# Attention weights loaded during the experts, split ahead of h, and the class norm solved together with tiles 0 to 3

## The chip, the core and the metric

The kernel runs on one core of a Trainium2 chip. A core has five engines, each with its own queue of instructions: TensorE (PE in the rows; its weight loads are PEld), VectorE (DVE), ScalarE (ACT), GpSimd (POOL) and SyncE (SP). They meet only through semaphores. Sixteen DMA engines serve all queues. The metric is the device time of one execution in microseconds (us).

## The reference

The program is a small vision tower with two layers. It works on h, 16 sequences of 129 rows (one class row and 128 tokens) of 512 numbers in float32.

```python
h = tokens of a state-space kernel, with the class row in front
h = h + scan_attention(layernorm(h))          # layer 0
h = h + experts(layernorm(h), H=256)          # layer 0: 8 experts, top 2, one shared expert
h = h + gla(layernorm(h))                     # layer 1, this case
h = h + experts(layernorm(h), I=352)          # layer 1
```

The change lies where the first line of experts ends and the line of `gla` begins. Of the latter:

```python
q = silu(x @ Wq.T) * SCALE
k_sig = sigmoid(x @ Wk.T)
gf = log_sigmoid(-k_sig)
o = gla(q, k_sig, x, gf)                      # a gated linear recurrence over the row index
go = o @ Wog.T + x @ Wig.T
rms = o * rsqrt(mean(o * o) + EPS) * g_weight
out = rms * go * sigmoid(go)
```

Here x is the layernorm of h. Wog and Wig are 512 x 512.

## The kernel before

h lies in the chip's memory as 17 tiles: tile n (0 to 15) holds the 128 tokens of sequence n, one to a partition, and tile 16 (`NB`) holds the 16 class rows. Each stage is a function that returns one piece of program for each engine; `tower` strings these together, so each engine runs the stages in the order tokenizer, scan, first experts (`ffn_layer`, "ffn0"), gated linear attention (`gla_layer`), second experts. The order of the work is thus the order of the code on each engine, and no scheduler changes it.

**The end of the first experts.** Rows are sorted by expert into 40 tiles (`NTILE`) of 128 slots. For each slot tile GpSimd gathers the rows, TensorE makes the products, VectorE scales the result, and GpSimd adds it with an accumulating scatter (L1514) into h in DRAM (`h_rows`). The semaphore `ffn0_e_down` counts the slot tiles that TensorE has finished. Expert weights lie over the place of the old norm output and beyond; SyncE loads experts 2 to 7 one after another (L990, L992) and then, as each pair has landed, counts up a semaphore that releases it. `stored` (L1139 to L1144) makes SyncE wait until the last scatter has landed in DRAM.

**The start of the attention.** SyncE (`sync` of `gla_layer`) first waits for the last product of the experts, since the weights wqk, wog, wig and the mask lie over memory that the experts used, then issues five loads, then waits in `stored`, and then loads h back: class rows first (L1847), then four quarters of four tiles (L1849). VectorE clears its buffers, copies three small pieces (`own`, L1862), and takes the norm in the groups of L1831: class tile, tiles 0 to 3, 4 to 9, 10 to 15. For each group it takes statistics (L495), aggregates (L519), solves the inverse root in nine dependent steps on all columns of the group (`newton`, L529 to L539) and applies the result tile by tile (L544), which counts up `gla_xn_ready`. TensorE turns each tile (L555) in that order and projects (L2112) the class rows and the quarters to queries and keys; ScalarE evacuates the turned tiles (L2029) and makes the bands (L2035 to L2042).

**The split.** For near-float32 products wog and wig are split in two parts: a rounded one, made by ScalarE (`s.activation(to[:, 0], w, ACT.Copy)`, L2017), and the rest, made by VectorE (a subtraction, L1877). Before, ScalarE does this first of all in the stage, and VectorE after all four groups of the norm. The first user is TensorE's `xw_of(0)`, which waits for all four parts (`gla_weights_split` 4).

Memory: `gla_raw` holds the unsplit weights and the mask, `gla_rounded` the parts and what else is rounded. Both begin at `y_at` before, `gla_raw` first.

## Time and profile before

| | |
|---|---|
| time, median of 3 runs | 1547.92 us (1547.54 to 1548.44) |
| the profiled execution | 1549.41 us, of which span 1547.6 us |
| PE busy | 1385.4 us, 90% of the span |
| PEld busy | 1078.2 us, 70% |
| DVE busy | 832.9 us, 54% |
| POOL busy | 483.6 us, 31% |
| ACT busy | 378.7 us, 24% |
| chain that ended last | PE 80%, DVE 11%, issue 3%, DMA 2%, ACT 2% |
| mean granted TensorE clock | 0.973 |

The span is the time from the first to the last record of the profile; what the execution's time has more lies around it. The busy shares are averages over stages that differ much. The chain follows the last instruction back, at each step to what released it, so it tells at each moment which engine the end of the program depended on. TensorE holds the chain over most of the run, with gaps at the seams between stages. The seam of this case lies between 600 and 700 us of the span.

### The profile page before, as it was taken

To read this page: it belongs to the slowest core of one execution; us is meant where nothing else is said; L and a number is where in the kernel's file an instruction comes from. 1 tells how busy PE (TensorE), PEld (TensorE's weight loads), DVE (VectorE), ACT (ScalarE), POOL (GpSimd) and SP (SyncE) were. 2 spreads that over 40 slices of the span, in tenths; PEclk is the share of its full clock that TensorE was granted. 3 is DMA by queue.
4 is the path that set the end of the run, shared out by engine and by line. 5 is a ranking of instruction groups with operands and counts; after the bars stand their busy time and mean duration, and the time that the engine had idled before them with its cause. 6 is when DMAs were issued, how large, how long until landed. Compare 5 with 4: busy or idle time off the path is not lost.

```text
span 1547.6 us, 21953 instructions
## 1 busy us (share of the span) xinstructions
PE 1385.4 (90%) x6469; PEld 1078.2 (70%) x6470; DVE 832.9 (54%) x1692; ACT 378.7 (24%) x738; POOL 483.6 (31%) x350
## 2 busy tenths in 40 slices
PE   0586939999999999389998989999999989999997
PEld 0584427888444444147776778888888879999996
DVE  8985898555222222663657765555555543333332
ACT  3114133121111111242223312333332212222221
POOL 0651530450344443001111035533323213343332
PEclk9999969999999999699999999999999999999999
DMA  4592007103955554600000504666665679676443
GB/s 102 112 153 24 1 22 266 34 10 116 342 93 89 89 94 62 195 22 1 1 0 1 185 21 133 204 215 209 216 224 200 222 272 372 208 206 187 75 74 42
DMA packets 88403, 197.04 MB, mean 127 GB/s; under 512 B 28256, under 2 KB 32224, under 8 KB 84832
## 3 DMA queue, kind: packets, MB, share of 16 engines
q1 hardware_dynamic: 68240, 154.20, 30.8%
q0 software_dynamic: 20096, 42.02, 14.7%
q8 instruction: 33, 0.54, 0.1%
q14 instruction: 34, 0.28, 0.1%
HBM read 112.24 MB, written 81.02 MB: 125 GB/s over the span
## 4 chain that ended last, share of the span: by engine, by line
PE 80%; DVE 11%; issue 3%; DMA 2%; ACT 2%; POOLq 1%; POOL 0%; DVEq 0%; SPq 0%; ACTq 0%
PE ps L1616 25%; PE ps L1676 19%; PE ps L1738 9%; PE ps L2143 6%; PE ps L1764 4%; PE ps L442 4%; PE ps L1706 2%; PE ps L555 2%; DVE held L495 1%; PE ps L1752 1%; PE ps L2112 1%; PE ps L2168 1%; PE ps L861 1%; PE ps L862 1%; DVE held L1383 1%
## 5 line engine op out<-in xcount | busy, mean ns | idle before, releaser
L1676 PE MATMUL ps<-moe_rounded 128*128 128x384 f32 (+2 forms) x1800 | 375.3, 351 | 0.0
L1676 PEld LDWEIGHTS ps<-moe_rounded 128*128 128x128 f32 x1800 | 326.9, 188 | 33.4
L1383 DVE SCALAR_TENSOR_TENSOR held<-ps,moe_scratch,held 128x512 f32<-128x512 f32 (+1 forms) x255 | 187.4, 747 | 180.0 <-PE ps L1616 179.2
L1616 PE MATMUL ps<-moe_expert_parts,moe_rows_parts 128*128 (+1 forms) x1320 | 256.5, 347 | 3.1 <-DVE moe_rows_parts L1407 1.5
L1616 PE MATMUL ps<-moe_rounded 128*128 128x512 f32 (+3 forms) x885 | 241.8, 393 | 11.8 <-DVE moe_rounded L1365 9.7
L1616 PEld LDWEIGHTS ps<-moe_expert_parts,moe_rows_parts 128*128 128x128 f32 (+1 forms) x1320 | 217.5, 188 | 16.3 <-issue 4.1
L1616 PEld LDWEIGHTS ps<-moe_rounded 128*128 128x128 f32 (+2 forms) x885 | 146.5, 171 | 50.7 <-DVE moe_rounded L1365 12.0
L1393 DVE TENSOR_TENSOR moe_scratch<-moe_scratch,ps 128x256 f32<-128x256 f32 (+1 forms) x80 | 37.7, 471 | 237.4 <-ACT moe_scratch L1598 237.4
L1738 PE MATMUL ps<-moe_experts,moe_scratch 128*128 x320 | 144.2, 593 | 0.6 <-issue 0.6
L1487 POOL TENSOR_TENSOR moe_split_parts<-moe_scratch,moe_split_parts 128x704 fp32r<-128x704 f32 (+2 forms) x48 | 88.8, 1855 | 172.8 <-ACT moe_split_parts L1580 172.8
L1471 POOL DMA_INDIRECT slot_tokens<-moe_scratch x68 | 73.5, 1081 | 173.2 <-DVE held L1383 165.9
L1598 ACT ACTIVATE moe_scratch<-ps 128x256 f32<-128x256 f32 (+1 forms) x80 | 33.9, 424 | 331.3 <-PE ps L1738 193.0
L1567 ACT ACTIVATE moe_scratch<-ps 128x384 f32<-128x384 f32 (+2 forms) x75 | 38.7, 515 | 307.7 <-PE ps L1676 298.5
L442 PE MATMUL ps<-sb 128*128 128x64 f32 x256 | 56.5, 422 | 54.6 <-DVE sb L367 54.3
L2143 PE MATMUL ps<-gla_rounded 128*128 128x512 f32 (+1 forms) x408 | 101.5, 406 | 2.1 <-ACT gla_rounded L2066 2.1
L1738 PEld LDWEIGHTS ps<-moe_experts,moe_scratch 128*128 128x128 f32 x320 | 57.7, 190 | 58.8 <-issue 58.8
L442 PEld LDWEIGHTS ps<-sb 128*128 128x128 f32 x256 | 55.2, 332 | 55.4 <-POOL sb L392 54.0
L2143 PEld LDWEIGHTS ps<-gla_rounded 128*128 128x128 f32 (+1 forms) x408 | 75.2, 187 | 22.2 <-issue 2.6
L2012 POOL TENSOR_TENSOR moe_xn<-moe_scratch 128x512 f32<-128x512 f32 (+1 forms) x17 | 25.6, 1506 | 195.7 <-DVE moe_scratch L1946 195.7
L555 PE MATMUL ps<-held,moe_xn 128*128 128x128 f32 (+1 forms) x272 | 40.4, 293 | 51.3 <-DVE moe_xn L544 45.7
L555 PEld LDWEIGHTS ps<-held,moe_xn 128*128 128x128 f32 (+1 forms) x272 | 33.7, 153 | 65.5 <-issue 31.4
L1764 PE MATMUL ps<-moe_experts,moe_scratch 128*128 x160 | 75.4, 593 | 1.1 <-DVE moe_scratch L1415 1.1
(315 smaller groups left out, 1690.1 us busy)
## 6 DMA issues: line engine op xcount, KB each, us to landing
moe_expert_parts<-expert_parts SPq DMA_DIRECT2D x8, 3840.0 KB, 13.0
expert_parts<-moe_split_parts SPq DMA_DIRECT2D x32, 704.0 KB
moe_scratch<-in_ffn_gate_up SPq DMA_DIRECT2D x32, 352.0 KB, 4.3
xn_rows<-moe_xn SPq DMA_DIRECT2D x2, 4096.0 KB, 13.0
moe_experts<-in_ffn_gate_up SPq DMA_DIRECT2D x8, 1024.0 KB, 15.5
expert_parts<-moe_split_parts SPq DMA_DIRECT2D x8, 1024.0 KB
moe_scratch<-in_ffn_sh_gate_up SPq DMA_DIRECT2D x15, 512.0 KB, 3.5
tokens<-sb SPq DMA_DIRECT2D x16, 256.0 KB
```

The costliest lines, as they stand in the source:

```text
L442: mm = t.matmul(o, ub[:, u, hh, :], bb[:, u, hh, :], start=True, stop=True)
L555: ins = t_eng.transpose(ps_bank[:, k * r:(k + 1) * r], xn[0:r, t, k * P:(k + 1) * P], ident[0:r, 0:r])
L1383: v.scalar_tensor_tensor(out=hb[0:rows, t, :], in0=ps[0:rows, ADDED[t % 3], :], scalar=sg[0:rows, t:t + 1], in1=hb[0:rows, t, :], op0=ALU. ...
L1393: v.tensor_tensor(ehid[:, u], esil[:, u], e_up(u), ALU.mult).then_inc(ehr, 1)
L1471: p.indirect_dma_start(out=slots, out_offset=bass.IndirectOffsetOnAxis(ap=pos_u[0:r, j, t:t + 1], axis=0), in_=tab_u[0:r, t, j, :], in_off ...
L1487: p.tensor_tensor(part[0:rows, x, 1, 0:w], raw[0:rows, x, 0:w], part[0:rows, x, 0, 0:w], ALU.subtract).then_inc(plr, 1)
L1567: s.activation(unit_sil(u, m), unit_banks(u, m)[0], ACT.Silu).then_inc(silr, 1)
L1616: mm = t.matmul(out, lhs(k, x), rhs(k, y), start=(k == 0 and i == 0), stop=(k == ks - 1 and i == 2))
L1676: mm = t.matmul(unit_banks(u, m)[j], weights(k, x, j), xT[y][:, k, unit_cols(m)], start=(k == 0 and i == 0), stop=(k == KD - 1 and i == 2))
L1738: mm = t.matmul(ps[:, u, 0:2 * F], xgT[:, u, k], exg(e, k, 0, 2 * F), start=(k == 0), stop=(k == KD - 1))
L1764: mm = t.matmul(ps[:, 6 + u, :], ehT[0:FR[f], u, f, :], exd(e, f, FR[f]), start=(f == 0), stop=(f == NF - 1))
L2143: mm = t.matmul(out[0:r], xT[:, j % 2, x, k, 0:r], w[:, y, k, :], start=(k == 0 and i == 0), stop=(stop and k == KD - 1 and i == 2))
```

## The change

Five edits, all at this seam:

1. The loads of wqk, wog, wig and the mask become a function `weights`, which SyncE runs inside the first experts' stage, right behind the load of expert 7 (`beside(sp)`), and no longer after the last product. The load of `g_weight` stays in `sync` and goes behind the five loads of h.
2. For that, `gla_raw` moves to memory that no expert weight uses, just below the scratch area, and `gla_rounded` takes its place at `y_at`.
3. ScalarE waits for four loads in place of five, and for the last product of the experts, before it writes the rounded parts.
4. VectorE does the two subtractions ahead of the norm.
5. The norm's groups are class tile and tiles 0 to 3 together, 4 to 9, 10 to 15. The tiles of the first group are no contiguous range, so its nine steps run on all 17 columns.

```diff
--- before.py
+++ after.py
@@ -518,7 +518,7 @@
             r = tile_rows(t)
             c.put(v.bn_aggr(self.mv[0:r, t, :], self.stats[0:r, t, :]))
         c.wait()
-        cols = slice(tiles[0], tiles[-1] + 1)
+        cols = slice(tiles[0], tiles[-1] + 1) if tiles[-1] >= tiles[0] else slice(0, T)
         self.newton(v, c, self.mv[:, cols, 1], 1.0, eps, cols)
 
     NEWTON = 9
@@ -886,7 +886,7 @@
     return rows[0:NTOK, :].rearrange("(b s) d -> s b d", s=SEQ)
 
 
-def ffn_layer(nc, sem, sb, ps, d, dram, g, name, F, NSH, before, xr, made, split_w):
+def ffn_layer(nc, sem, sb, ps, d, dram, g, name, F, NSH, before, xr, made, split_w, beside=None):
 
 
 
@@ -1132,6 +1132,7 @@
         else:
             for e in range(2, NE):
                 load_expert(sp, e, e_in[e // 2])
+            beside(sp)
             for k in range(1, NE // 2):
                 sp.wait_ge(e_in[k], 2 * 16 * WD)
                 sp.sem_inc(rt, 1)
@@ -1788,7 +1789,7 @@
     return sync, vector, gpsimd, scalar, tensor, stored, ed
 
 
-def gla_layer(nc, sem, sb, ps, d, hd, h_in, h_got, g, before, stored, xr_next, rest):
+def gla_layer(nc, sem, sb, ps, d, hd, h_in, h_got, g, before, experts_done, stored, xr_next, rest):
 
 
 
@@ -1799,10 +1800,10 @@
     KH, BL, NBL, NG = 32, 32, 4, 4
     ROWS3 = 2 * KH + NB
     xn = Arena(g.low).take(T, D)
-    raw = Arena(g.gla_raw, g.y_at, g.y_at)
+    raw = Arena(g.gla_raw, g.gla_raw_at, g.gla_raw_at)
     wqk, wog, wig = raw.take(KD, 2 * KH), raw.take(KD, D), raw.take(KD, D)
     mask = raw.take(P)
-    f = Arena(g.gla_rounded, raw.at, raw.at)
+    f = Arena(g.gla_rounded, g.y_at, g.y_at)
     wo, wi = f.take(2, KD, D), f.take(2, KD, D)
     xT = f.take(2, 2, KD, P)
     atcF, xc3, xwc3, accF = f.take(NB, P), f.take(D), f.take(D), f.take(NG * P)
@@ -1810,7 +1811,7 @@
     kb = a.take(NBL, NG, SEQ)
     qr, sq, kk, av, bv, pv = (a.take(NG, SEQ) for _ in range(6))
     kcz, own, ss, xg16 = a.take(NBL, ROWS3), a.take(NB), a.take(T), a.take(KD, NB)
-    assert a.at <= g.high_at
+    assert a.at <= g.gla_raw_at
     a = Arena(g.high, g.high_at, g.high_at)
     xg = a.take(2, KD, QC)
     sg, pb, xw, ats, junk, gw = a.take(2, D), a.take(2, D), a.take(2, D), a.take(2, P), a.take(D), a.take(D)
@@ -1828,25 +1829,28 @@
     hr = sem("gla_h_ready")
 
     ORDER = [NB] + list(range(NB))
-    GROUPS = ([NB], range(0, 4), range(4, 10), range(10, NB))
+    GROUPS = (ORDER[0:5], ORDER[5:11], ORDER[11:T])
     TB1, CLS_BANK, QK_BANKS = (0, 1, 2), 3, (4, 5, 6, 7)
     TB2, XW_BANK, AT_BANK, ACC_BANK, O_BANKS, G_BANKS = (0, 1), 2, 3, 5, (4, 5), (6, 7)
     C3_ALL = 8
     bands = [slice(KH * q, KH * q + KH) for q in range(NG)]
     rows_of = (lambda n: NB if n == NB else P)
 
-    def sync(sp):
-        before(sp)
+    def weights(sp):
         sp.dma_start(wqk, d["Wqk"]).then_inc(w_in, 16)
         sp.dma_start(wog, d["Wog"].rearrange("(k p) n -> p k n", p=P)).then_inc(w_in, 16)
         sp.dma_start(wig, d["Wig"].rearrange("(k p) n -> p k n", p=P)).then_inc(w_in, 16)
-        sp.dma_start(gw, d["g_weight"].partition_broadcast(P)).then_inc(w_in, 16)
         sp.dma_start(mask, d["causal"]).then_inc(w_in, 16)
+
+    def sync(sp):
+        before(sp)
         stored(sp)
         hd_rows = by_sequence(hd)
         sp.dma_start(hb[0:NB, NB, :], hd_rows[0]).then_inc(h_in[NQ], 16)
         for q in range(NQ):
             sp.dma_start(hb[:, 4 * q:4 * q + 4, :], hd_rows[1:SEQ, 4 * q:4 * q + 4]).then_inc(h_in[q], 16)
+        sp.wait_ge(w_in, 4 * 16)
+        sp.dma_start(gw, d["g_weight"].partition_broadcast(P)).then_inc(w_in, 16)
 
     def vector(v):
         c = norm.chain(v)
@@ -1860,6 +1864,9 @@
         c.wait()
         for j in range(3):
             c.put(v.tensor_copy(own[KH * j:KH * j + NB], ident[KH * j:KH * j + NB, KH * j:KH * j + NB]))
+        v.wait_ge(wsp, 2)
+        for w, to in ((wog, wo), (wig, wi)):
+            v.tensor_tensor(to[:, 1], w, to[:, 0], ALU.subtract).then_inc(wsp, 1)
         for tiles in GROUPS:
             for n in tiles:
                 if n % NQ == 0:
@@ -1872,9 +1879,6 @@
         v.wait_ge(xr, 1)
         v.wait_ge(c3, 4)
         v.tensor_tensor(xc3[KH:KH + NB], xn[0:NB, NB, :], xc3[0:NB], ALU.subtract).then_inc(c3, 1)
-        v.wait_ge(wsp, 2)
-        for w, to in ((wog, wo), (wig, wi)):
-            v.tensor_tensor(to[:, 1], w, to[:, 0], ALU.subtract).then_inc(wsp, 1)
 
         def low_part(j):
             n = ORDER[j]
@@ -2012,7 +2016,8 @@
             p.tensor_tensor(xn[0:r, n, :], pb[0:r, j % 2], gw[0:r], ALU.mult).then_inc(gwr, 1)
 
     def scalar(s):
-        s.wait_ge(w_in, 5 * 16)
+        s.wait_ge(w_in, 4 * 16)
+        s.wait_ge(*experts_done)
         for w, to in ((wog, wo), (wig, wi)):
             s.activation(to[:, 0], w, ACT.Copy).then_inc(wsp, 1)
 
@@ -2103,7 +2108,7 @@
             gate(j)
 
     def tensor(t):
-        t.wait_ge(w_in, 5 * 16)
+        t.wait_ge(w_in, 4 * 16)
 
         def project(q):
             w, bank = (NB, CLS_BANK) if q < 0 else (QC, QK_BANKS[q])
@@ -2220,7 +2225,7 @@
                 xw_of(j + 1)
             outs(j)
 
-    return sync, vector, gpsimd, scalar, tensor, qk
+    return sync, vector, gpsimd, scalar, tensor, qk, weights
 
 
 ROUNDED = 2 * KD * NTOK + 448 + 4 * (2 * KD * P + D) + 4 * QC
@@ -2278,8 +2283,9 @@
         self.split_parts = over("moe_split_parts", self.xn_at, self.xn_at + SPLIT, F32R)
         self.rows_at = max(self.xn_at + PARTS, self.high_at)
         self.rows_parts = over("moe_rows_parts", self.rows_at, self.rows_at + ROWS, F32R)
-        self.gla_raw = over("gla_raw", self.y_at, self.y_at + GLA_RAW)
-        self.gla_rounded = over("gla_rounded", self.y_at + GLA_RAW, self.y_at + GLA_RAW + GLA_ROUNDED, F32R)
+        self.gla_raw_at = self.high_at - 2 * 2 * 2 * P - GLA_RAW
+        self.gla_raw = over("gla_raw", self.gla_raw_at, self.gla_raw_at + GLA_RAW)
+        self.gla_rounded = over("gla_rounded", self.y_at, self.y_at + GLA_ROUNDED, F32R)
         self.high = over("moe_scratch", self.high_at, WORDS)
 
 
@@ -2305,8 +2311,8 @@
         xn_ready = [sem(f"ffn{k}_xn_ready") for k in range(2)]
         tok = tokenizer(nc, sem, sb, ps, d, h0, g.h, h_in, [*g.weights_loaded, g.parts_stored[0]], g.parts_stored[1:])
         scan = scan_layer(nc, sem, sb, ps, d, h_in, g, g.scratch_at)
-        ffn0 = ffn_layer(nc, sem, sb, ps, d, dram, g, "ffn0", 256, 4, scan[5], xn_ready[0], None, False)
-        gla = gla_layer(nc, sem, sb, ps, d, dram["h"], h_in, H_LOADED, g, lambda sp: sp.wait_ge(ffn0[6], NTILE), ffn0[5], xn_ready[1], gla_rest)
+        ffn0 = ffn_layer(nc, sem, sb, ps, d, dram, g, "ffn0", 256, 4, scan[5], xn_ready[0], None, False, lambda sp: gla[6](sp))
+        gla = gla_layer(nc, sem, sb, ps, d, dram["h"], h_in, H_LOADED, g, lambda sp: sp.wait_ge(ffn0[6], NTILE), (ffn0[6], NTILE), ffn0[5], xn_ready[1], gla_rest)
         ffn1 = ffn_layer(nc, sem, sb, ps, d, {**dram, "h": out}, g, "ffn1", 352, 11, lambda sp: sp.wait_ge(gla[5], 5), xn_ready[1], gla_rest, True)
         block = ctx.enter_context(nc.Block())
```

SyncE's queue, from the last expert's load to the first load of the next stage. Before:

```order
L992 DMA moe_experts<-in_ffn_down 128x2x512
L1840 DMA gla_raw<-in_Wqk 128x256
L1841 DMA gla_raw<-in_Wog 128x4x512
L1842 DMA gla_raw<-in_Wig 128x4x512
L1843 DMA moe_scratch<-in_g_weight 128x512
L1844 DMA gla_raw<-in_causal 128x128
L1847 DMA held<-h_rows 16x512
L1849 DMA held<-h_rows 128x4x512 x4
L1046 DMA moe_scratch<-in_ffn_router 128x36
```

and now:

```order
L992 DMA moe_experts<-in_ffn_down 128x2x512
L1840 DMA gla_raw<-in_Wqk 128x256
L1841 DMA gla_raw<-in_Wog 128x4x512
L1842 DMA gla_raw<-in_Wig 128x4x512
L1843 DMA gla_raw<-in_causal 128x128
L1849 DMA held<-h_rows 16x512
L1851 DMA held<-h_rows 128x4x512 x4
L1853 DMA moe_scratch<-in_g_weight 128x512
L1046 DMA moe_scratch<-in_ffn_router 128x36
```

The four weight loads now stand in the queue without a wait between them and the experts' loads; before, the first of them (L1840) waits for the last product and for all expert weights. The wait for the scatters stands at the class rows' load in both (L1847, now L1849).

VectorE's queue, from its last small copy (`own`, L1862, now L1866), with the semaphores that a row waits for. `h_loaded4` is the class rows, `h_loaded0` the first quarter. Before:

```order
L1862 COPY sb<-held 16x16 x2
L495 BN_STATS held<-held 16x6 [waits h_loaded4]
L519 BN_AGGR held<-held 16x2 [waits norm_chain]
L529 TENSOR_SCALAR held<-held 128x1 [waits norm_chain]
...
L539 SCALAR_TENSOR_TENSOR held<-held 128x1 [waits norm_chain]
L544 TENSOR_SCALAR moe_xn<-held 16x512 [waits norm_chain]
L495 BN_STATS held<-held 128x6 [waits h_loaded0]
L495 BN_STATS held<-held 128x6 x3
L519 BN_AGGR held<-held 128x2 [waits norm_chain]
...
L544 TENSOR_SCALAR moe_xn<-held 128x512 x5
L1874 TENSOR_TENSOR gla_rounded<-moe_xn,gla_rounded 16x512 [waits gla_cls_operands_ready,gla_xn_ready]
L1877 TENSOR_TENSOR gla_rounded<-gla_raw,gla_rounded 128x2048 [waits gla_weights_split]
```

and now:

```order
L1866 COPY sb<-held 16x16 x2
L1869 TENSOR_TENSOR gla_rounded<-gla_raw,gla_rounded 128x2048 [waits gla_weights_split]
L1869 TENSOR_TENSOR gla_rounded<-gla_raw,gla_rounded 128x2048
L495 BN_STATS held<-held 16x6 [waits h_loaded4]
L495 BN_STATS held<-held 128x6 [waits h_loaded0]
L495 BN_STATS held<-held 128x6 x3
L519 BN_AGGR held<-held 16x2 [waits norm_chain]
L519 BN_AGGR held<-held 128x2 x4
L529 TENSOR_SCALAR held<-held 128x17 [waits norm_chain]
...
L544 TENSOR_SCALAR moe_xn<-held 16x512 [waits norm_chain]
L544 TENSOR_SCALAR moe_xn<-held 128x512 x4
```

The two 128x2048 subtractions have moved from behind the last group to ahead of the class rows' statistics, with their wait for `gla_weights_split`. The class tile's own nine steps and its early apply are gone; its statistics, its aggregate and its apply (16x512) stand in the first group, the apply ahead of those of tiles 0 to 3.

## Rows read from the trace of the kernel before

**Rows 1.** The chain of waits, 600 to 700 us (start, us, what).
```profile
622.63 9.12 DMA h_rows<-held,moe_scratch
...
632.32 5.38 DMA held<-h_rows
637.72 2.49 DVE held L495 x4
...
651.64 5.60 PE ps L2112 x8
...
660.22 3.58 PE ps L2112 x8
```

**Rows 2.** Timeline of SyncE's queue, 363 to 700 us (start, us, engine, line, what).
```profile
395.39 6.04 SPq L990 DMA_DIRECT2D moe_experts<-in_ffn_gate_up  x1
...
621.59 0.33 SPq L1840 DMA_DIRECT2D gla_raw<-in_Wqk  x1
```

**Rows 3.** Timeline of GpSimd, in four stretches (start, us, engine, line, what, idle before).
```profile
416.73 1.58 POOL L1514 DMA_INDIRECT h_rows<-held,moe_scratch  x1 [1.85 <-DVE held L1402]
...
422.74 1.59 POOL L1514 DMA_INDIRECT h_rows<-moe_scratch  x1 [2.06 <-DMA h_rows<-held,moe_scratch]
...
596.79 1.57 POOL L1514 DMA_INDIRECT h_rows<-held,moe_scratch  x1 [3.64 <-DVE held L1402]
...
801.93 1.28 POOL L2012 TENSOR_TENSOR moe_xn<-moe_scratch 128x512 f32<-128x512 f32 x1 [8.02 <-DVE moe_scratch L1946]
...
1539.19 1.55 POOL L1514 DMA_INDIRECT out<-held,moe_scratch  x1 [2.81 <-DMA out<-held,moe_scratch]
```

**Rows 4.** Windows (busy us of PE, PEld, DVE, ACT, POOL; PE clock, DMA share, GB/s).
```profile
420.00:426.00 6.00, 6.00 (x20) 2.92 (x19) 1.57 (x4) 1.11 (x3) 2.77 (x3) 1.00 0.74 170
601.00:601.50 0.50, 0.50 (x4) 0.41 (x3) 0.00 (x0) 0.00 (x0) 0.00 (x0) 1.00 0.10 16
630.00:631.00 1.00, 0.00 (x0) 0.00 (x0) 0.00 (x0) 0.00 (x0) 0.00 (x0) 0.50 1.05 344
655.00:656.00 1.00, 1.00 (x3) 0.37 (x2) 1.00 (x2) 0.00 (x0) 0.00 (x0) 0.70 0.00 0
1543.00:1543.50 0.50, 0.00 (x0) 0.00 (x0) 0.00 (x0) 0.00 (x0) 0.00 (x0) 0.57 0.47 78
1543.50:1544.00 0.50, 0.00 (x0) 0.00 (x0) 0.00 (x0) 0.00 (x0) 0.00 (x0) 0.50 0.03 4
```

**Rows 5.** Timeline of ScalarE, from 634 us.
```profile
634.24 1.91 ACT L2017 ACTIVATE gla_rounded<-gla_raw 128x2048 fp32r<-128x2048 f32 x1 [17.30 <-DMA gla_raw<-in_causal]
```

**Rows 6.** DMA issues, 560 to 660 us (KB each, median us to landing).
```profile
held<-h_rows SPq DMA_DIRECT2D x1, 32.0 KB, 2.4
```

**Rows 7.** Timeline of VectorE, in four stretches.
```profile
624.41 0.49 DVE L1862 COPY sb<-held 16x16 f32<-16x16 f32 x3
634.40 0.68 DVE L495 BATCH_NORM_STATS2 held<-held 16x6 f32<-16x512 f32 x1 [9.50 <-DMA held<-h_rows]
...
637.05 0.53 DVE L544 TENSOR_SCALAR moe_xn<-held 16x512 f32<-16x512 f32 x1
...
662.71 4.49 DVE L1877 TENSOR_TENSOR gla_rounded<-gla_raw,gla_rounded 128x2048 fp32r<-128x2048 f32 x2
677.83 0.23 DVE L1883 TENSOR_TENSOR gla_rounded<-ps,gla_rounded 128x64 fp32r<-128x64 f32 x1 [10.63 <-ACT gla_rounded L2066]
...
801.97 1.27 DVE L530 TENSOR_SCALAR held<-held 128x4 int32<-128x4 int32 x1
```

**Rows 8.** Groups of instructions of VectorE, shapes apart (busy us, mean ns).
```profile
L537 DVE TENSOR_TENSOR held<-held 128x4 f32<-128x4 f32 x7 | 1.2, 165 | 0.2
...
L537 DVE TENSOR_TENSOR held<-held 128x17 f32<-128x17 f32 x2 | 0.4, 178 | 0.1
```

**Rows 9.** Timeline of TensorE, 633 to 640 us.
```profile
637.74 0.58 PE L555 MATMUL ps<-held,moe_xn 16*128 16x16 f32 x4 [16.18 <-DVE moe_xn L544]
```

## Prediction

> **What bounds the kernel now.** I read the chain of waits first, between 600 and 700 us [rows 1], because every edit acts at the seam between the first expert layer and the attention layer. Over most of the run the chain lies on TensorE; at this seam it leaves it. TensorE ends its last expert product at 621.6 (SyncE waits for the same semaphore and goes on at 621.59, [rows 2]). Then [rows 1] show one accumulating scatter of rows into h, 9.12 us from 622.63, and after it the first quarter of h coming back, 5.38 us from 632.32. At 637.72 VectorE starts the statistics of tiles 0 to 3. Only from there do TensorE and ScalarE take over again. So the time is set by two transfers in a row, and an edit here is worth what it takes from those two or from VectorE's work behind them.
>
> Why does the scatter take 9.12? I looked next for the same instruction elsewhere. GpSimd's scatter of 596.79 has no load beside it: the traffic has nearly gone by 601.0 to 601.5 (share 0.10). The last one of the kernel, from 1539.19, is over in the slice 1543.5 to 1544.0 (0.03), where it still had 0.47 half a microsecond before [rows 3, 4]. Both last about 4.4 us. In the 9.12 us case the sixteen DMA engines carry 344 GB/s at 630 to 631, their share 1.05 [rows 4]: the 2.5 MB of attention weights issued from 621.59 on. They are still landing at 634.24, when ScalarE's wait for the last of them ends [rows 5], so they also overlap the beginning of h's return.
>
> **The change, part by part.**
>
> Weights loaded during the experts. Wqk, Wog, Wig and the mask (128 + 1024 + 1024 + 64 KB, 2.3 MB) go behind the last expert's load on SyncE's queue, at about 403; only g_weight (256 KB) stays near the seam, and it is now behind h's five loads. The last scatter then has the DMA engines nearly alone. I take 4.4 us for it, saving 4.7. Bounds: 4.2 us (saving 4.9) from the alone cases, and 6.0 us (saving 3.1) from the scatter of 416.73, under the expert loads, which the next scatter waits for until 422.74 [rows 3]. The first quarter of h: the class rows, 32 KB, land in a median of 2.4 us after issue [rows 6]; 1.05 MB at the 344 GB/s of [rows 4] is 3.05 us; together 5.4, with a faster rate and some overlap less. I take 5.0, saving 0.4, bounds 0 and 1.3.
>
> What these loads cost where they now are: 2.3 MB at 344 GB/s is 6.7 us more of heavy traffic, between about 422 and 430. There TensorE is busy 6.00 of 6.00 us, the DMA engines' share is 0.74 [rows 4], and a scatter that waited 2.06 us for the one before [rows 3] did not stop it. SyncE itself may stand longer at issue (one load there already took 6.04 us to issue, [rows 2]); what it has to do behind them is to release experts 2 to 7, whose turn comes tiles later. I take 0, bounds 0 and 0.5.
>
> The split beside the loads. ScalarE's two rounded copies (1.91 us each, [rows 5]) start at 621.6, not 634.24, and end at 625.4. VectorE has finished its own small copies at 624.9 [rows 7], waits 0.5 us for them, and does the two subtractions (4.49 us together, [rows 7]) until 629.9. This adds a wait to VectorE; queued behind it is all of the norm, for which TensorE waits. By the sums above the scatter lands at 627.0. The first quarter is issued 0.6 us behind that landing (631.75 to 632.32 now), at 627.6, and lands at 632.6; the class rows go out just before it and land by 630.0. So the cover is the scatter plus h's return: VectorE takes the class statistics (0.68 us, [rows 7]) by 630.7 and still waits 1.9 us. If h came more than 1.9 us sooner than I think, VectorE would be the late one, and the gain could not exceed 637.72 - 630.7 - 0.8 = 6.2 us. Where the subtractions came from they cost nothing: VectorE idles 10.63 us before its next work at 677.83 [rows 7]. There the removal is worth 0, from both sides.
>
> The class norm solved with tiles 0 to 3. The separate class solve lasts 3.2 us, from the statistics at 634.40 to the end, at 637.58, of the 0.53 us apply from 637.05 [rows 7]. That is just before the first quarter arrived, so its removal is worth 0 as things are. With the new times it would have been late: 630.0 + 3.2 = 633.2 against 632.6, 0.6 us. What it puts onto the path: one more aggregate, 0.1; nine steps on 17 columns in place of 4, 9 x (178 - 165) ns = 0.1 [rows 8]; the class apply, 0.53, ahead of tile 0's, and TensorE's turn of the class tile, 0.58 [rows 9], ahead of tile 0's turn. Since VectorE applies tile 0 while TensorE turns the class tile, these last two cost 0.6 and not 1.1. Sum 0.8, bounds 0.5 and 1.2. ScalarE's evacuation of the class tile moves likewise.
>
> A cost looked for behind the numbers: VectorE and GpSimd can hold each other up. At 801.97 a step on four columns takes 1.27 us, where such steps take 165 ns [rows 8], while GpSimd's addition runs from 801.93 for 1.28 us [rows 3, 7]. The scatter of 622.63 ends on GpSimd at 624.2 (1.55 us long in the like row of 1539.19, [rows 3]), 1.2 us before the first subtraction begins, so I put nothing for it.
> The Trainium skill, SBUF — State Buffer, section "SBUF: two separate sides", warns that a GpSimd DMA looks blocked while VectorE holds the port they share, because its descriptors cannot be written; the section "Who interferes with whom" adds that a VectorE instruction with two SBUF inputs excludes a GpSimd instruction that reads SBUF. The row at 801.97 agrees that one waits for the other; no row shows a scatter held up. By that rule alone, if descriptors were still being written at 625.4, the scatter would gain nothing: that is a rival below.
>
> **Sum.** -4.7 (scatter) - 0.4 (first quarter) + 0 (experts) + 0 (split) + 0.8 (class tile on the path) = -4.3 us. Behind 637.72 everything should shift as it is: project, turns and bands are chained on TensorE and ScalarE, and the main attention loop is paced by TensorE. The sum is made against the profiled execution, span 1547.6, 1549.41 with what lies around it; 1545.1 by that. This execution is 1.5 us above the median of the runs, 1547.92. I apply the difference to the median: **1543.6 us**.
>
> **The rivals.**
> 1. *The scatter keeps other company.* It lands in 6.0 us, as the one of 416.73 did: -3.1 - 0.4 + 0.8 = -2.7, 1545.2. For it: g_weight and the small router loads remain; against: all of them now stand behind h's loads on the same queue, thus after the scatter. Chance 0.08.
> 2. *The clock falls otherwise.* After the idle time TensorE's granted clock is half (1.2 of 2.4 GHz); it rises within 655 to 656 (mean 0.70, [rows 4]), after four microseconds of unbroken products. The projection that spans the rise takes 5.60 us, the next, all at full clock, 3.58 [rows 1]. A rise before it would save 2.0 (1541.6), none during it would cost about 1.6 (1545.2). The change joins the class turn to the others (TensorE is busy 0.58 us longer in one piece ahead of its next pause), which speaks slightly for the first; later short dips may also move, either way. Chances 0.12 for better, 0.11 for worse.
> 3. *VectorE holds the scatter's descriptors* (other side: slower). If they wait until the subtractions end at 629.9, and the transfer then needs the 2.6 us that traffic lasts in the alone case, it lands at 632.5 in place of 631.75: +0.8 - 0.4 + 0.8 = +1.2, 1549.1. It decides as soon as descriptor writing reaches past 625.4; GpSimd's record ends before. Chance 0.04.
> 4. *The weights delay the experts.* If all 6.7 us of their traffic reached TensorE: +2.4, 1550.3; with a late release of an expert more. It needs rows gathered later than some three tiles ahead. TensorE unbroken at 420 to 426 speaks against. Chance 0.03.
> 5. *The change doesn't do what it says*: the 9.12 us have another cause than the weights, and only the 0.8 remains, 1548.7. The two alone cases speak against. Chance 0.02.
>
> **How the numbers follow.** The forecast has 0.60. Its own range, from the bounds (3.1 to 4.9, 0 to 1.3, 0 to 0.5, 0.5 to 1.2, not all at one end), is 1542.4 to 1545.0. With rival 2 on both sides and rival 1 the range for 8 in 10 is 1541.3 to 1546.0. A measurement of this kernel tells about 0.2%, 3.1 us, from no change: faster by more means below 1544.8. Of the forecast 0.57 of 0.60 lies there, all of the better clock, 0.04 of the worse, 0.03 of rival 1: 0.76. Slower than 1551.0 needs rival 4 at its full price or beyond it: 0.03. The rest, 0.21, is within.
>
> **What would show it.** In the chain of the changed kernel the scatter should last 4.2 to 4.9 us and the first quarter 4.1 to 5.4; ScalarE's two copies should start within 0.3 us of the last expert product and VectorE's two subtractions end before the class rows' statistics; VectorE should wait some 1.9 us for the first quarter, after the class statistics; TensorE should be unbroken from 400 to 616; statistics to tile 0's first turn should be 0.8 us longer than now. I am wrong if the scatter stays above 6 us, if VectorE's wait ends by ScalarE and not by a DMA, or if TensorE has a gap behind the expert loads.

## The result

The changed kernel takes 1543.43 us (median of 8 executions, 1540.31 to 1545.92) against 1547.73 us for the kernel before, run beside it: ratio 0.9973, 95% interval 0.9963 to 0.9983, or 4.3 us less. In microseconds the interval is 2.6 to 5.7. Repeated among the experiments, on two chips, it gave 0.9961 [0.9947, 0.9975] and 0.9973 [0.9960, 0.9987]. The forecast was 1543.6 us. The profiled execution took 1541.11 us (span 1539.2), which is 8.3 us below the one shown of before; the next section says how much of that is the change.

### The profile page after: what moved, and what is told of

Read it like the earlier page. It is cut to its first block, busy times and chain, and to the rows that moved or that the text cites. A ratio compares the mean times of both kernels' runs of the same rounds, so it can differ in the third digit from the quotient of the medians.

```text
span 1539.2 us, 21945 instructions
## 1 busy us (share of the span) xinstructions
PE 1379.2 (90%) x6469; PEld 1075.0 (70%) x6470; DVE 831.1 (54%) x1683; ACT 378.9 (25%) x738; POOL 483.5 (31%) x350
## 4 chain that ended last, share of the span: by engine, by line
PE 80%; DVE 11%; issue 3%; ACT 2%; DMA 2%; POOLq 1%; POOL 0%; DVEq 0%; SPq 0%; ACTq 0%
PE ps L1617 25%; PE ps L1677 19%; PE ps L1739 9%; PE ps L2148 6%; PE ps L1765 4%; PE ps L442 4%; PE ps L1707 2%; PE ps L555 2%; PE ps L1753 1%; PE ps L2117 1%; DVE held L495 1%; PE ps L2173 1%; PE ps L861 1%; PE ps L862 1%; PE ps L796 1%
## 5 line engine op out<-in xcount | busy, mean ns | idle before, releaser
L2148 PE MATMUL ps<-gla_rounded 128*128 128x512 f32 (+1 forms) x408 | 99.3, 399 | 3.3 <-ACT gla_rounded L2071 2.1
L2148 PEld LDWEIGHTS ps<-gla_rounded 128*128 128x128 f32 (+1 forms) x408 | 74.2, 185 | 22.5 <-ACT gla_rounded L2071 2.3
```

Source lines behind the costliest of these rows:

```text
L2148: mm = t.matmul(out[0:r], xT[:, j % 2, x, k, 0:r], w[:, y, k, :], start=(k == 0 and i == 0), stop=(stop and k == KD - 1 and i == 2))
```

## The profile after

In the changed kernel the lines of the attention stage are four or five higher: L1402 is now L1403, L2112 is L2117. The chain of waits over the seam (start us, us, what), to be laid beside [rows 1]:

```profile
619.75 0.76 DVE held L1403
620.78 4.55 DMA h_rows<-held,moe_scratch
625.54 0.33 SPq L1849
625.92 5.34 DMA held<-h_rows
631.29 2.48 DVE held L495 x4
633.79 0.44 DVE held L519 x5
...
636.17 0.54 DVE moe_xn L544
636.85 3.33 PE ps L555 x16
...
645.75 6.15 PE ps L2117 x8
651.90 2.97 PE ps L555 x24
654.87 3.58 PE ps L2117 x8
```

The scatter has gone from 9.12 to 4.55 us. The first quarter of h takes 5.34 us, as before (5.38). Behind it the aggregates are five, and TensorE turns 16 pieces in one go where it turned 4 and then 12. The projection at 645.75 lasts 6.15 us (5.60 before).

The loads now stand on SyncE's queue behind the experts' (timeline; start, us), and the windows (busy us of PE, PEld, DVE, ACT, POOL; PE clock, DMA share, GB/s) show what they do there:

```profile
399.69 1.24 SPq L992 DMA_DIRECT2D moe_experts<-in_ffn_down  x1
400.98 4.35 SPq L1840 DMA_DIRECT2D gla_raw<-in_Wqk  x1
405.37 0.89 SPq L1841 DMA_DIRECT2D gla_raw<-in_Wog  x1
406.30 7.08 SPq L1842 DMA_DIRECT2D gla_raw<-in_Wig  x1
413.42 5.92 SPq L1843 DMA_DIRECT2D gla_raw<-in_causal  x1
```

```profile
420.00:426.00 6.00, 6.00 (x19) 2.84 (x18) 1.77 (x5) 0.98 (x2) 2.58 (x2) 1.00 1.06 350
426.00:432.00 6.00, 6.00 (x20) 3.01 (x19) 1.77 (x6) 0.98 (x2) 2.56 (x2) 1.00 0.99 236
432.00:438.00 6.00, 6.00 (x19) 2.87 (x19) 1.76 (x6) 0.98 (x2) 2.57 (x2) 1.00 0.50 84
```

The DMA share of 420 to 426 rises from 0.74 in [rows 4] to 1.06, and TensorE is still busy all of the time. SyncE stood 18 us over four issues, and nothing waited for it.

ScalarE and VectorE at the seam (timeline, with the idle time before each and what ended it):

```profile
619.81 3.71 ACT L2022 ACTIVATE gla_rounded<-gla_raw 128x2048 fp32r<-128x2048 f32 x2 [4.71 <-PE ps L1765]
```

```profile
623.55 4.49 DVE L1869 TENSOR_TENSOR gla_rounded<-gla_raw,gla_rounded 128x2048 fp32r<-128x2048 f32 x2 [0.49 <-ACT gla_rounded L2022]
627.97 0.68 DVE L495 BATCH_NORM_STATS2 held<-held 16x6 f32<-16x512 f32 x1
631.29 2.47 DVE L495 BATCH_NORM_STATS2 held<-held 128x6 f32<-128x512 f32 x4 [2.64 <-DMA held<-h_rows]
...
672.48 0.23 DVE L1887 TENSOR_TENSOR gla_rounded<-ps,gla_rounded 128x64 fp32r<-128x64 f32 x1 [15.64 <-ACT gla_rounded L2071]
```

ScalarE's copies begin with the last product, VectorE's subtractions end ahead of the class rows' statistics, and a DMA still ends VectorE's wait, after 2.64 us. Where the subtractions were, the idle time has grown from 10.63 to 15.64 us [rows 7]: it was free there.

**Of the 8.4 us between the two spans, the seam holds 3.9.** 1.9 us are already there at the last scatter (622.63 against 620.78), ahead of the first changed instruction that is waited for. They are no part of the change: with the same loads early, this scatter starts between 620.17 (e12) and 623.65 us (e8) in the profiles of the experiments. The statistics of tiles 0 to 3 stand 6.4 us earlier (637.72, 631.29), thus 4.6 are won by then. From the start of the last scaled result to the end of the first turns it is 20.43 us, and it was 24.27: 3.84 won. The rest, 2.7 us, arises later, with fewer stretches at half clock: before there are 3.4 us of it from 679.5 and 6.8 us from 696.6, after only 3.4 us from 691.8. That measure, "the seam" below, leaves out all that comes before and behind, and a few tenths of a microsecond show in it where the median does not tell them.

## The experiments

Ratios are to the kernel before, run on the same chip in the same rounds, with 95% intervals. Three chips served: one for e1, e2, e3 and e6, another for e5, e7, e8 and e9, the third for e4, e10, e11 and e12. Each edit is shown against the changed kernel. Each kernel has one profile, so a seam is a single reading: the changed kernel's three are 20.43, 20.57 and 20.60 us.

### Only the loads moved (e1_loads_only)

The subtractions stay behind the norm and the class tile is solved apart.

```diff
+    GROUPS = (ORDER[0:1], ORDER[1:5], ORDER[5:11], ORDER[11:T])
-    GROUPS = (ORDER[0:5], ORDER[5:11], ORDER[11:T])
...
-        v.wait_ge(wsp, 2)
-        for w, to in ((wog, wo), (wig, wi)):
-            v.tensor_tensor(to[:, 1], w, to[:, 0], ALU.subtract).then_inc(wsp, 1)
         for tiles in GROUPS:
...
         v.tensor_tensor(xc3[KH:KH + NB], xn[0:NB, NB, :], xc3[0:NB], ALU.subtract).then_inc(c3, 1)
+        v.wait_ge(wsp, 2)
+        for w, to in ((wog, wo), (wig, wi)):
+            v.tensor_tensor(to[:, 1], w, to[:, 0], ALU.subtract).then_inc(wsp, 1)
```

> The kernel before with the early weight loads alone: VectorE subtracts after the last group, and the class tile is solved by itself. Theory (the weights' traffic is the whole gain): the last scatter 4.5 us, the first quarter 5.3, as in the changed kernel; the class solve (3.2 us from some 1.7 us after its load is issued) ends before the first quarter lands, so from that landing to the end of the first turns it takes 8.2 us as before, not 8.9; total 1542.7, 0.7 below the changed kernel. Rival (the split ahead of h and the joined class solve carry part of the gain): the subtractions at about 656 to 660 now hold TensorE's first split product, or the class solve holds tile 0; total 1544.5 to 1546.5.

Measured: 1543.89 us, 0.9981 [0.9970, 0.9992]. The scatter took 4.57 us, the quarter 5.35, the seam 19.71. Its VectorE timeline:

```profile
628.86 0.68 DVE L495 BATCH_NORM_STATS2 held<-held 16x6 f32<-16x512 f32 x1 [4.19 <-DMA held<-h_rows]
...
631.51 0.53 DVE L544 TENSOR_SCALAR moe_xn<-held 16x512 f32<-16x512 f32 x1
632.92 2.47 DVE L495 BATCH_NORM_STATS2 held<-held 128x6 f32<-128x512 f32 x4 [0.87 <-DMA held<-h_rows]
...
657.90 4.49 DVE L1881 TENSOR_TENSOR gla_rounded<-gla_raw,gla_rounded 128x2048 fp32r<-128x2048 f32 x2
```

The move of the loads alone wins all that the seam wins: 24.27 to 19.71, which is 0.7 us better than the whole change. With the split out of the way VectorE finishes the class tile and still waits 0.87 us. So the local part of the theory held; the time was expected at 1542.7 and came at 1543.89.

### The class tile solved apart (e2_class_apart, e12_class_apart_again)

```diff
+    GROUPS = (ORDER[0:1], ORDER[1:5], ORDER[5:11], ORDER[11:T])
-    GROUPS = (ORDER[0:5], ORDER[5:11], ORDER[11:T])
```

> The changed kernel with the class tile solved by itself again. The prediction on record: the class solve would end 0.6 us after the first quarter's landing, so from that landing to the end of the first turns it takes 8.2 + 0.6 = 8.8 us, and nothing is won or lost against 8.9. Rival, from the changed kernel's own profile (VectorE is free at 628.0, waits 2.64 us for the first quarter at 631.29): the class solve ends at 631.2, just hidden, and the stretch takes 8.2 to 8.3; total 0.6 below the changed kernel's, 1542.8.

> The changed kernel with the class tile solved apart, as before. If the local stretch decides (19.8 us against 20.4), it is 0.6 us below the changed kernel; if the clock behind the first projection decides, it is 1 to 2 us above, as the two were the first time.

Measured: 1544.66 us, 0.9987 [0.9977, 0.9997]; the second time 1543.67 us, 0.9978 [0.9967, 0.9989]. Seam 19.78 and 20.17 (the scatter and the quarter took 4.86 and 5.53 us there). VectorE in the first of them:

```profile
630.78 0.67 DVE L495 BATCH_NORM_STATS2 held<-held 16x6 f32<-16x512 f32 x1
...
633.42 0.53 DVE L544 TENSOR_SCALAR moe_xn<-held 16x512 f32<-16x512 f32 x1
634.20 2.47 DVE L495 BATCH_NORM_STATS2 held<-held 128x6 f32<-128x512 f32 x4 [0.24 <-DMA held<-h_rows]
```

Split, class solve and class apply just fit in front of the quarter: a DMA still ends the wait, 0.24 us (0.63 in the second). Solved apart, the class tile costs the path nothing; joined it costs 0.7 us from the quarter's landing to the end of the first turns (8.88 us against 8.14). So the rival of this expectation held locally, and the step of the forecast that had the class solve 0.6 us late did not. But the median does not follow: apart was not below joined either time. That is taken up behind the last experiment.

### The split behind the norm (e3_split_last)

The edit is that of e1_loads_only without its first pair of lines.

> The changed kernel with VectorE's two subtractions back behind the last group. Theory (they are hidden in both places): the first quarter's landing, the first turns and the start of the first split product stay as they are, total 1543.4 within noise; VectorE waits some 7 us for h where it waited 2.64. Rival (they now take VectorE's time where TensorE waits): first split product later by up to 4.5 us, total up to 1548.

Measured: 1542.68 us, 0.9973 [0.9963, 0.9984]; seam 20.49 (20.43 in the changed kernel). VectorE waits 4.32 and 3.28 us for the two landings in place of 0 and 2.64. With early loads it is worth nothing where the split stands.

### The loads back at the seam (e6_loads_late)

```diff
-            beside(sp)
...
         before(sp)
+        weights(sp)
         stored(sp)
```

> The changed kernel with the four weight loads back at the seam, ahead of the scatter's wait (the split still ahead of the norm, the class tile still joined). Theory: the last scatter is back at 8.5 to 9.2 us; and the split, which needs the last weight, now stands in front of the norm: ScalarE copies from 10 to 12 us after the last product until 3.8 later, VectorE subtracts 4.5, so the first quarter's statistics start 4 to 5 us after it has landed; total 1552 to 1553.5, slower than before by 4 to 5. Rival (the scatter was slow for another reason): scatter 4.5 us, total about 1548.

Measured: 1551.97 us, 1.0038 [1.0025, 1.0051]; seam 29.12. GpSimd issued the scatter at 622.72, and SyncE went on to load h at 631.88; with the 0.21 us that lie between a landing and that load in the changed kernel, the scatter took 9.0 us. The chain of waits:

```profile
623.16 10.00 DMA gla_raw<-in_causal
633.19 3.72 ACT gla_rounded L2022 x2
636.93 4.50 DVE gla_rounded L1869 x2
641.42 2.97 DVE held L495 x5
```

The early split needs the early loads: without them ScalarE's copies and VectorE's subtractions stand one behind the other on the path, and the seam is 4.9 us longer than before (0.7 of it the joined class tile's). The cover that the prediction named for the split (the scatter plus h's return) is real, and it is gone when the weights come late.

### One of the loads back at the seam (e4_wig_again)

```diff
-        sp.dma_start(wig, d["Wig"].rearrange("(k p) n -> p k n", p=P)).then_inc(w_in, 16)
...
         before(sp)
+        sp.dma_start(wig, d["Wig"].rearrange("(k p) n -> p k n", p=P)).then_inc(w_in, 16)
         stored(sp)
```

> One of the moved loads, the 1 MB Wig, goes back to the seam, ahead of h's return on SyncE's queue. If the scatter's 9.12 us came from the loads it shares the DMA engines with, it now lies between the two cases: an estimate by bytes, 4.55 + (9.12 - 4.55) x 1.0 / 2.4 = 6.5 us. ScalarE's rounded copies wait for Wig (some 5 to 6 us after the last product), VectorE's subtractions follow and the first quarter of h finds VectorE still busy by about 1 us: first statistics some 3 us later than in the changed kernel, total about +3 on it. The rival says that it is not the bytes but the number of loads or their first ones that hold the scatter: then it stays at 4.5 us or goes to 9.

Measured: 1549.86 us, 1.0018 [1.0005, 1.0030]; seam 25.90. Chain, then SyncE's waits (longest wait in the last column) and its queue:

```profile
622.06 8.27 DMA gla_raw<-in_Wig
630.35 3.72 ACT gla_rounded L2022 x2
634.09 4.49 DVE gla_rounded L1869 x2
638.59 2.98 DVE held L495 x5
```

```profile
SPq L1143 <- DMA h_rows<-held,moe_scratch: 9.2, 1, 9.2
```

```profile
622.06 0.37 SPq L1846 DMA_DIRECT2D gla_raw<-in_Wig  x1
631.82 0.33 SPq L1849 DMA_DIRECT2D held<-h_rows  x1
```

The size that was expected, 6.5 us by bytes, failed, and so did the time, about 3 us above the changed kernel; of the rival, 4.5 or 9 us, the second is nearly it. In the changed kernel SyncE goes on to load h 0.21 us after the scatter's landing; by that the scatter, issued at 623.10, landed at 631.6 here, 8.5 us. So 1 MB of loads costs 4.0 of the 4.6 us that 2.5 MB cost: here the price is far from proportional to the bytes. The load itself took 8.27 us, 127 GB/s, where 1 MB of h took 5.34 us. This kernel loses even against the one before. Of the 5.5 us by which its seam exceeds the changed kernel's, the scatter is 4.0; the other 1.5 come since the early split waits for Wig, so VectorE starts the five statistics late, one behind the other. What one load at the seam costs with the split behind the norm was not run.

### VectorE at work while the scatter is issued (e5_port)

An extra subtraction, wog less wig, goes into a buffer that is overwritten later. It stands ahead of VectorE's first clear, where GpSimd issues the scatter.

```diff
         c = norm.chain(v)
+        v.wait_ge(w_in, 4 * 16)
+        c.link(v.tensor_tensor(wo[:, 1], wog, wig, ALU.subtract))
         c.put(v.memset(ss, 1.0))
```

> The changed kernel with one more subtraction of two memory operands (128x2048, 2.25 us, its result is overwritten later) on VectorE right behind the last scaled result, so that it runs while GpSimd issues the last scatter. Rival 3 of the prediction (VectorE holds up the scatter's descriptors): GpSimd's scatter record grows from 1.55 to some 3.5 us or starts 2 us later, and the scatter, 4.55 us, lands 2 us later, in 6.5 us. Theory (they don't meet in a way that counts): scatter record 1.55, landing 4.5 us after it; VectorE's own work ends 2.3 us later, which its wait of 2.64 us for the first quarter still covers, total as the changed kernel.

Measured: 1546.71 us, 0.9988 [0.9978, 0.9998], where the changed kernel on this chip had 0.9961. GpSimd's timeline, then VectorE's:

```profile
620.85 3.35 POOL L1515 DMA_INDIRECT h_rows<-held,moe_scratch  x1 [1.77 <-DVE held L1403]
```

```profile
620.49 2.28 DVE L1858 TENSOR_TENSOR gla_rounded<-gla_raw 128x2048 fp32r<-128x2048 f32 x1
...
633.16 2.47 DVE L495 BATCH_NORM_STATS2 held<-held 128x6 f32<-128x512 f32 x4 [2.59 <-DMA held<-h_rows]
```

The GpSimd instruction lasts 3.35 us where it lasts 1.55 in the changed kernel: it ends 1.43 us after VectorE's subtraction does. The scatter lands after 6.54 us (4.91 in e9, on the same chip), and the seam is 22.23 (20.57). So the mechanism of rival 3 exists, with a price of 1.7 us. The Trainium skill, SBUF — State Buffer, section "Who interferes with whom", states that a VectorE instruction with two inputs in SBUF contends with a GpSimd instruction that reads SBUF. The 3.35 us agree with that. The changed kernel does not pay it, since its first subtraction starts at 623.55, 1.2 us after GpSimd's record has ended. The median is 3.7 us above that of e9, so 2 us lie outside the seam. All 8 executions of e5 had a mean granted clock under 0.976; the section "Where the seam's gain goes" takes that up, and against the executions of the changed kernel with such a clock (five, mean 1545.2) e5 (1546.6) is 1.5 us longer, about the price at the seam.

### The first quarter in four loads (e7_four_loads, e8_four_class_apart, e10_four_apart_last), the changed kernel beside them (e9_changed_again, e11_changed_third)

```diff
+        for n in range(NQ):
+            sp.dma_start(hb[:, n:n + 1, :], hd_rows[1:SEQ, n:n + 1]).then_inc(lone[n][0], 16)
-        for q in range(NQ):
+        for q in range(1, NQ):
             sp.dma_start(hb[:, 4 * q:4 * q + 4, :], hd_rows[1:SEQ, 4 * q:4 * q + 4]).then_inc(h_in[q], 16)
...
-                if n % NQ == 0:
+                if n < NQ:
+                    v.wait_ge(lone[n][0], lone[n][1] + 16)
+                elif n % NQ == 0:
                     v.wait_ge(h_in[n // NQ], h_got[n // NQ] + 16)
```

e8 adds the edit of e2, and e10 those of e2 and e3.

> The changed kernel once more, beside the next three, for a comparison on one chip. Against before 0.9973, as it was (4.2 us). If the joined class tile is what makes the kernels with it faster than those without (0.9973 and 0.9973 against 0.9981 and 0.9987 so far, although the stretch from the first quarter's landing to the end of the first turns is 0.7 us longer with it), the same again, and the records show TensorE at half clock for less time between 600 and 720 us; if that was luck of the clock, this one lands near 0.998.

> The changed kernel with the first quarter of h loaded as four loads of one tile each, with a semaphore each. Theory (VectorE's four statistics, 2.48 us, need not wait for the whole megabyte): tile 0 lands some 3 us after its issue and each further tile 0.7 us later, the statistics (0.62 us each) run along, and they end 0.7 to 1.0 us behind the last of the four, so 1.2 to 1.8 us earlier than now, counted from the scatter's landing; total 1.5 below the changed kernel. Rival (the loads of a queue share the engines, so all four land together, or three more issues at 0.5 us each make the last one late): statistics start when they did, nothing won or 0.5 lost.

> As the one before, with the class tile solved by itself. By the sum: the class solve (3.2 us from 628.0 or later) would now end behind tile 0's landing, VectorE is the late one by 1 to 2 us, and the gain of the four loads is lost: statistics of tile 0 start where they do in the changed kernel; total as the changed kernel, or up to 1 above by the clock. Rival: the first tiles land no earlier, class solve hidden, 0.7 below the changed kernel.

> The early loads as in the changed kernel, but the class tile is solved apart, the two subtractions stay behind the norm, and the first quarter of h comes in as four loads of one tile. VectorE is then free and each piece waits for DMA only. Theory (class solve hidden, 0.7 us of the joined tile off the path, 0.3 us from the four loads): from the start of the last scaled result to the end of the first turns 19.2 us, against 20.4 in the changed kernel; total about 1 us below the changed kernel on this chip. Rival (the joined class tile is worth its cost because the pause before the first projection is arranged otherwise and the clock rises earlier): local stretch shorter, total the same or above.

> The changed kernel once more, so that the class tile joined and apart are timed on one chip in the same rounds. Both theories: 0.997 of the kernel before.

| kernel | time, us | ratio [95%] | seam, us |
|---|---|---|---|
| e9, changed | 1543.04 | 0.9961 [0.9947, 0.9975] | 20.57 |
| e7, four loads | 1542.81 | 0.9965 [0.9952, 0.9979] | 20.32 |
| e8, four, class apart | 1542.55 | 0.9959 [0.9945, 0.9973] | 19.45 |
| e11, changed | 1542.14 | 0.9973 [0.9960, 0.9987] | 20.60 |
| e10, four, apart, split last | 1542.96 | 0.9971 [0.9960, 0.9981] | 19.05 |

VectorE in e7:

```profile
631.08 1.34 DVE L495 BATCH_NORM_STATS2 held<-held 128x6 f32<-128x512 f32 x2 [0.33 <-DMA held<-h_rows]
634.40 1.36 DVE L495 BATCH_NORM_STATS2 held<-held 128x6 f32<-128x512 f32 x2 [1.98 <-DMA held<-h_rows]
```

Tile 0 has landed by 631.1 and tile 2 only at 634.4, so half of the statistics is done early. But counted from the scatter's start tile 2 comes 11.5 us behind it, and the whole quarter came after 10.65 us in e9: what the early half saves (1.1 us of statistics) is nearly lost again, and 0.25 us is won of the 1.2 to 1.8 expected. In e8 VectorE becomes the late engine (its chain goes over ScalarE's copies, the subtractions and the class solve). In e10, without the split in front, the class statistics begin with the landing of the class rows, but from there VectorE is again the one that is late: no landing ends a wait of it at the four tiles, against the expectation that each piece would wait for DMA only.

```profile
622.98 4.81 DMA h_rows<-held,moe_scratch
...
628.00 1.71 DMA held<-h_rows
629.74 0.69 DVE held L495
...
632.93 2.42 DVE held L495 x4
```

The seam of e10 was expected at 19.2 and came at 19.05. The time was expected 1 us below the changed kernel and came 0.8 above, within the intervals. No version was found that can be told from the changed kernel on the fast side.

### Where the seam's gain goes

The kernels with the class tile apart have a seam 0.3 to 1.5 us shorter and are not faster. I followed two later marks, from the start of the last scaled result: the start of the first block of 24 products of 128 rows in the attention loop (L2148; at 679.72 in the changed kernel), and that of the block after the next half block (699.85).

| | seam | first block | later block | PE clock 690 to 700 |
|---|---|---|---|---|
| changed | 20.4 | 59.97 | 80.10 | 0.83 |
| e11, changed | 20.6 | 60.04 | 80.16 | 0.83 |
| e9, changed | 20.6 | 60.42 | 82.99 | 0.54 |
| e3, joined | 20.5 | 59.77 | 79.87 | 0.83 |
| e7, four, joined | 20.3 | 59.93 | 80.06 | 0.83 |
| e12, apart | 20.2 | 59.75 | 79.88 | 0.83 |
| e1, apart | 19.7 | 59.56 | 82.11 | 0.50 |
| e2, apart | 19.8 | 59.79 | 82.31 | 0.56 |
| e8, four, apart | 19.5 | 59.61 | 80.56 | 0.66 |
| e10, four, apart | 19.1 | 59.31 | 80.28 | 0.66 |

About half of a gain at the seam is gone by the first block. The projection of the first quarter begins at half clock, and in these kernels and e5 that half clock ends 30.8 to 31.7 us after the start of the last scaled result, whether the seam is 19.05 us long or 22.2. (The time of a rise follows from the mean clock of the 1 us window that holds it: 0.59 in 650 to 651 of the changed kernel puts it at 650.8, 0.57 in 652 to 653 of e10 at 652.9, 0.53 in 650 to 651 of e5 at 650.9.) Who comes to the projection sooner does more of it at half clock: 6.66 us in e10 (rise 6.1 us after its start), 6.15 in the changed kernel (5.1), 5.18 in e5 (3.1). Of the 1.4 us of e10 0.7 are left. For the whole change it is the same: the half clock ended after 34.0 us before and after 31.1 now, the projection grew from 5.60 to 6.15 us, and at the first products of the attention loop (678.15 before, 672.81 now) 3.5 of the 3.84 us are left.

Then comes a step that goes with the clock of the window: from the first mark to the second it is 20.1 us at 0.83, 21.0 at 0.66, and 22.5 to 22.6 at 0.50 to 0.56. The windows of the changed kernel and of e2, with the columns as above:

```profile
690.00:700.00 10.00, 9.36 (x40) 7.03 (x40) 3.22 (x7) 3.05 (x7) 1.27 (x1) 0.83 0.01 2
```

```profile
690.00:700.00 10.00, 10.00 (x30) 6.41 (x30) 5.40 (x7) 1.86 (x4) 1.26 (x1) 0.56 0.01 2
```

The trace has 40 products of TensorE in these 10 us at a mean clock of 0.83 and 30 at 0.56. A like difference shows over all executions. Joined (the changed kernel three times and e3), the mean granted clock of the execution was 0.976 or more in 24 of 31; apart (e1, e2, e12), in 11 of 34. The mean times were 1542.85 and 1544.09 us, 1.24 apart, 95% interval 0.3 to 2.1. On one chip and in the same rounds it is 1.8 [0.5, 3.1] (e3 against e1 and e2) and 1.1 [-0.6, 2.8] (e11 against e12). Within either clock group they agree: 1542.2 and 1542.1 at 0.976 or more, 1545.1 and 1545.1 below. The kernel before had 30 of 72 in the upper group, and means of 1545.5 and 1548.7, so at like clock the change is worth 3.3 and 3.5 us. The bound of 0.976 was chosen with these figures at hand. And the kernels with four loads do not follow it: only 6 of the 20 executions of e7, e8 and e10 were at 0.976 or more, yet their mean is 1542.9 us, that of the joined ones. With them counted in, joined and apart are 0.8 [0.0, 1.6] us apart.

So the joined class tile costs 0.7 us at the seam and came with the higher clock more often; in these executions it was not slower for it, and by the means faster by about a microsecond. Why, stays open. That the longer unbroken piece of turns (3.33 us for 2.82) brings it is not shown: no run changed TensorE's work alone, and e9 and e12 show that either kernel can have either clock.

## Why the prediction was right

- **Scatter.** Forecast -4.7 (4.4 us), measured -4.57 (4.55 us; 4.57 to 4.91 in the others with early loads, e5 aside). The cause holds: e1, which moves only the loads, has 4.57, and with loads back it was 8.5 (e4) and 9.0 us (e6).
- **First quarter.** Forecast -0.4, bound 0; measured -0.04. This was the mis-sized term. A latency of 2.4 and 3.05 us by rate made 5.4, which is what it takes; I then took 0.4 off for a faster rate and some overlap. The rate is faster (410 GB/s in the slice of 630 to 631), the class rows land sooner (1.7 us), and still the whole takes 5.1 to 5.5 us in the kernels with early loads. Why is not shown; four separate loads do not shorten it.
- **Experts.** Forecast 0, measured 0: TensorE is busy 18.00 of 18.00 us from 420 to 438, and from 400 to 616 it waits for no other engine.
- **Split.** Forecast 0 with 1.9 us of wait left, measured 0 with 2.64 left. e3 confirms that its place is worth nothing; e6 and e4 show what it costs when its cover is gone.
- **Class tile.** Forecast +0.8, measured +0.73. What was wrong is the reason beside it: solved apart it would be 0.6 us late. It is hidden (e2, 0.24 us to spare). From the scatter's start the class solve ends after 10.4 us in e2, near my sum (10.6), but the quarter lands after 10.6 and not after 10.0: the scatter took 4.77 us and not 4.4, the quarter 5.22 and not 5.0. So joining does not save a lateness; all of it is cost, at the seam. The +0.8 itself was reckoned from the rows and holds.
- **Sum.** -4.3 forecast; the seam gives -3.84, and the median -4.3. At like clock the executions give 3.3 to 3.5. The difference to 4.3 lies within the interval (2.6 to 5.7), and as far as it is real it goes with the clock, of which the forecast had only a rival (2, better by 2.0). Also wrong is that behind 637.72 everything shifts as it is: the projection took 0.55 us longer, and 3.5 us were left at the attention loop. That median and forecast agree to 0.2 us is luck: the optimistic quarter and the longer projection were made up for by the clock further on, which was not in the sum. The mechanism, two transfers in a row of which the first gets the DMA engines to itself, is what the runs show.
- **Rivals.** 1 fell (4.55 us, not 6.0). 3 is a real mechanism (e5), but here GpSimd's record has ended 1.2 us before the first subtraction begins. 4 and 5 fell. Of 2 neither half happened as it was put. The clock does rise early, at 640.6, while the class projection runs, but TensorE then waits for ScalarE, and it is half again from 644.0, before the projection of 645.75. That takes 6.15 us (it was 5.60), neither of the two times that the rival had (3.6 and 7.2). Nor does the rise come four microseconds after the projection's start: it came after 3.1 (e5) to 6.1 us (e10). The clock was better later on: 16 of 21 executions of the changed kernel had the upper clock, 30 of 72 of the one before.

## What to carry to other kernels

When a small transfer ends the path between two stages, look at what is issued beside it. Here one load of 1 MB cost nearly as much (4.0 us) as all 2.5 MB (4.6), so do not count on a gain by bytes when only some can be moved. A step put in front of a wait is free only as long as what it waits for is early too: price both cases. And where an edit is worth a microsecond, measure the stretch around it by itself, because the clock that follows can hide or double it in the median.

## What the runs showed of the hardware

- An accumulating scatter of 128 x 512 takes 4.55 to 4.91 us without bulk loads beside it, 8.5 beside one load of 1 MB (e4), 9.0 beside 2.3 MB (e6), 9.12 beside 2.5 MB (before); the 1 MB load beside it takes 8.27 us (e4).
- A VectorE subtraction of two operands over 128 x 2048 stretches GpSimd's issue of a scatter from 1.55 to 3.35 us (e5). Memsets and small copies there (620.46 to 623.1 in the changed kernel) leave it at 1.55 us.
- Of four loads of 256 KB the first had landed by 631.1 and the third at 634.4, 6.0 us after the first was issued (e7); one load of 1 MB takes 5.1 to 5.5 us.
- In the eleven profiles with all four weight loads early, TensorE's half clock under the projection of the first quarter ended 30.8 to 31.7 us after the start of the last scaled result, for seams of 19.05 to 22.2 us; in the kernel before after 34.0.
- Behind the experts' loads SyncE stood 4.35, 7.08 and 5.92 us at the issue of loads of 128 KB, 1 MB and 64 KB (L1840, L1842, L1843), and 0.89 us at one of 1 MB (L1841).
